# Selective scan: softplus passes on ScalarE by blocks of 512 columns instead of once over 1024

## The reference

```
xi, z = split(x @ inW.T);  u = silu(conv(xi) + convB)
dt, Bm, Cm = split(u @ xpW.T)
delta = softplus(dt @ dtW.T + dtB)            # 256 channels x 128 steps, 32 batches
A = -exp(Alog)                                # 256 channels x 16 states
h[t] = h[t-1] * exp(delta[t] * A) + delta[t] * u[t] * Bm[t]
y[t] = sum over the 16 states of h[t] * Cm[t]
out  = (y + u * Dp) * silu(z) @ outW.T
```

## Time and profile before

| | us |
|---|---|
| median of 3 runs | 3032.21 (3030.99 to 3034.59) |
| profiled execution, whole | 3035.91 |
| its span | 3033.8 |
| busy PE / DVE / ACT / POOL | 2180.6 / 2012.0 / 1294.2 / 1329.9 |

### The profile page before, as it was taken

How to read it: one execution, slowest core, us unless ns; L and a number is a source line. 1 busy time by engine, 2 the same in 40 slices (tenths; PEclk the granted TensorE clock), 3 DMA queues, 4 the chain that set the end, 5 groups by cost and what they waited for, 6 DMA issues and landing times. The chain is left out here.

```text
span 3033.8 us, 48820 instructions
## 1 busy us (share of the span) xinstructions
PE 2180.6 (72%) x19339; PEld 1337.4 (44%) x19339; DVE 2012.0 (66%) x3246; ACT 1294.2 (43%) x1935; POOL 1329.9 (44%) x1015
## 2 busy tenths in 40 slices
PE   3788766775266668998959999999999975552703
PEld 1354444554144545555525545545545543331303
DVE  3554455887444435555528888788888885888598
ACT  1344325554244422222237666666666642221460
POOL 2332243555323000000008899898898892332001
PEclk8899887887577879999979999999999997765856
DMA  3343000000343210000022222222222221000001
GB/s 90 72 77 62 10 17 31 17 17 3 73 82 75 38 47 1 1 1 1 1 62 74 71 81 80 73 75 81 78 74 73 77 63 32 21 8 8 0 0 28
DMA packets 136673, 134.58 MB, mean 44 GB/s; under 512 B 23664, under 2 KB 129920, under 8 KB 133248
## 3 DMA queue, kind: packets, MB, share of 16 engines
q1 hardware_dynamic: 136448, 131.47, 16.6%
HBM read 109.14 MB, written 15.99 MB: 41 GB/s over the span
## 5 line engine op out<-in xcount | busy, mean ns | idle before, releaser
L2154 POOL TENSOR_TENSOR mam_h<-mam_h,mam_c_all 128x1024 f32<-128x1024 f32 x256 | 658.7, 2590 | 87.9 <-DVE mam_h L2226 87.9
L2226 DVE TENSOR_TENSOR_SCAN mam_h<-mam_decay,mam_ps_b 128x1024 f32<-128x1024 f32 x256 | 574.4, 2274 | 97.2 <-PE mam_ps_b L1857 95.1
L1857 PEld LDWEIGHTS mam_ps_b<-mam_diag,mam_duT 64*128 64x128 f32 x4096 | 251.9, 190 | 219.8 <-DVE mam_h L2226 129.6
L2048 ACT ACTIVATE mam_decay<-mam_delta,mam_a_neg 128x508 f32<-128x508 f32 x512 | 331.3, 710 | 31.2 <-DVE mam_h L2226 26.9
L1857 PE MATMUL mam_ps_b<-mam_diag,mam_duT 64*128 64x128 f32 x4096 | 297.9, 287 | 55.2 <-DVE mam_h L2226 43.3
L737 DVE TENSOR_REDUCE at_top<-at_ps_s 128x8 f32<-128x1024 f32 x128 | 156.7, 1224 | 239.9 <-PE at_ps_s L483 239.7
L1876 PE MATMUL mam_ps_y<-mam_h,all_ident 64*64 64x512 f32 x2048 | 255.3, 614 | 11.9 <-POOL mam_h L2154 11.9
L620 ACT ACTIVATE at_e<-at_ps_e 128x1024 f32<-128x1024 f32 x128 | 131.2, 1025 | 194.3 <-PE at_ps_e L483 194.2
L1449 ACT ACTIVATE moe_silu<-moe_ps_g 128x512 f32<-128x512 f32 x144 | 86.0, 597 | 288.6 <-PE moe_ps_g L1396 262.2
L1399 PE MATMUL moe_ps_u<-moe_ynT,moe_w_up 128*128 128x512 f32 x288 | 158.6, 634 | 35.2 <-DVE moe_hidden L1532 35.2
L1532 DVE TENSOR_TENSOR moe_hidden<-moe_silu,moe_ps_u 128x512 f32<-128x512 f32 x144 | 96.9, 686 | 97.7 <-PE moe_ps_u L1399 94.0
(11 more groups left out here) (349 smaller groups left out, 4537.8 us busy)
## 6 DMA issues: line engine op xcount, KB each, us to landing
mam_c_all<-mam_c_rows SPq DMA_DIRECT2D x256, 256.0 KB, 3.4
at_rows<-at_split SPq DMA_DIRECT2D x64, 192.0 KB, 3.1
at_k<-at_rows SPq DMA_DIRECT2D x192, 64.0 KB
at_q<-at_rows SPq DMA_DIRECT2D x32, 192.0 KB
at_q<-at_rows SPq DMA_DIRECT2D x32, 128.0 KB
all_x_all<-in_x SPq DMA_DIRECT2D x8, 256.0 KB, 4.8
at_q<-at_rows SPq DMA_DIRECT2D x32, 64.0 KB
at_q<-at_tops SPq DMA_DIRECT2D x128, 6.0 KB
```

The costliest lines, as they stand in the source:

```text
L1857: last = nc.tensor.matmul(ps_b[:, slot, odd, :, at // 2, x:x + HT], duT[r, d, s % DT, at, :], diag[r, chunk % SLOTS, at, :, :], start=True ...
L2048: last = nc.scalar.activation(decay[:, s % SLOTS, :, n, :, 1:T], src, ACT.Exp, scale=a_neg[:, d, s % DT, st:st + 1])
L2154: nc.gpsimd.tensor_tensor(flat(h[:, slot, :, :, :, :]), flat(h[:, slot, :, :, :, :]), flat(c_all[:, chunk, :, :, :, :]), ALU.mult).then_in ...
L2226: nc.vector.tensor_tensor_scan(row(h[:, s % H_SLOTS, :, :, :, :]), row(decay[:, s % SLOTS, :, :, :, :]), row(ps_b[:, s % 2, :, :, :, :]), ...
```

## The change

For each channel block, as soon as its product is copied to `pre`, ScalarE makes Abs, Exp, the four squares and the positive part of that block (128 x 512); before, all this came once for both blocks behind the second copy. The positive part stands between the third and the fourth square instead of ahead of the first. The wait ahead of Abs for the copy is now there for each block. The exp is waited for directly ahead of the first square. ScalarE's step counter has 4 x DT counts a group instead of 4. Poly k still works on both blocks, and waits for square k of block 1.

```diff
@@ def softplus(f, steps, d, t, n)
-                if t == DT - 1:
-                    act.wait_ge(taken, f.base + f.n + ALL_TAKEN)
-                    steps.then(nc.scalar.activation(soft[:], pre[:], ACT.Abs))
-                    steps.settle()
-                    steps.then(nc.scalar.activation(soft[:], soft[:], ACT.Exp, scale=-1.0))
-                    nc.scalar.activation(pre[:], pre[:], ACT.Relu)
-                    steps.settle()
-                    for k in range(len(LOG1P_PAIRS)):
-                        nc.scalar.activation(square[:, k, :, :], soft[:], ACT.Square, bias=centre[:, k:k + 1]).then_inc(square_ready, 1)
+                act.wait_ge(taken, f.base + f.n + ALL_TAKEN)
+                steps.then(nc.scalar.activation(soft[:, t, :], pre[:, t, :], ACT.Abs))
+                steps.settle()
+                steps.then(nc.scalar.activation(soft[:, t, :], soft[:, t, :], ACT.Exp, scale=-1.0))
+                steps.settle()
+                for k in range(len(LOG1P_PAIRS)):
+                    if k == len(LOG1P_PAIRS) - 1:
+                        nc.scalar.activation(pre[:, t, :], pre[:, t, :], ACT.Relu)
+                    nc.scalar.activation(square[:, k, t, :], soft[:, t, :], ACT.Square, bias=centre[:, k:k + 1]).then_inc(square_ready, 1)
@@ def group(i, more, first=False)
-                steps = Steps(act, act_steps, i * 4 + 2, 4)
+                steps = Steps(act, act_steps, i * 4 * DT + 2 * DT, 4 * DT)
@@ def log1p(steps, n, part)
-                    dve.wait_ge(square_ready, n * len(LOG1P_PAIRS) + k + 1)
+                    dve.wait_ge(square_ready, (n * DT + DT - 1) * len(LOG1P_PAIRS) + k + 1)
```

## The result

The changed kernel is **slower by 0.64%**: ratio 1.0064, 95% interval 1.0050 to 1.0078, which is 15 to 24 us of 3033.4 (medians 3033.4 before and 3051.7 after, six runs each). The profiled execution took 3051.37 us, span 3049.2, against 3035.91 and 3033.8.

The account below looks back on a forecast made before the run. GpSimd was taken as the bound outside the softplus steps, with the chain to the first square setting when both engines go on; 2.0 + 5.5 + 4.8 + 2.0 = 14.3 us on 3032.21 gave 3046.5 us, range 3033 to 3065.

Parts of the forecast that it names:

- The chain: ScalarE's passes from copy 0 to the first square of block 1: 9.0 us against 6.97, so 2.04 us later.
- What gets through: Part of the 2.04 us shift that delays scan 9, the rest being hidden behind GpSimd's product of step 8.
- Second direction's halves: Six half groups of the pipelined loop preparing the second direction: scan 9 later by 0.34 us each, 2.0 together.
- Halves with the 4.9 us add: Five first direction's halves with the layer norm of the group before: scan 9 later by 1.1 us each, 5.5 together.
- First half: Half of the loop with poly 0 at 1622.27, taking 1.23 us, nothing hidden: +2.04 us.
- the odd halves: Four halves priced singly by poly 0's length: +2.04, +1.57, +1.2 and 0.0 us, together 4.8.
- The sum: All terms of the Mamba stage, loop halves and prologue, added: 14.3 us slower.
- The prologue: Before the loop, VectorE's wait for the first square: same longer chain, no GpSimd product to hide in, +2.0 us.
- Swallowed: Rival: VectorE's and GpSimd's collisions fall out otherwise, the time stays within 6 us, about 3035 us; chance 0.18.
- The whole shift gets through: Rival: nothing is hidden, 16 x 2.04 = 32.6 us slower, 3064.8 us; chance 0.15.
- Faster: Rival: the add ahead of the norm runs at once everywhere, shortening five halves, 3022 to 3030 us; chance 0.09.

Follow-up runs that it names:

- r3: Kernel before with one more positive part of 1024 columns ahead of the squares, not needed for the result; 1.0035 to the kernel before.
- r4: Changed kernel with two more positive parts of 512 columns in block 0, not needed for the result; 1.0107 to the kernel before.
- r8: The changed kernel itself, run again beside other kernels on the same chip; 1.0052 to the kernel before.
- r1: Kernel before with only the positive part moved behind the third square, passes whole; 1.0018 to the kernel before.
- r6: Changed kernel with the four polys a step later, behind scans 9 to 12 instead of 8 to 11; 1.0092 to the kernel before.
- r9: Changed kernel with VectorE's polys by blocks too, eight of 512 columns behind scans 8 to 11; 1.0244 to the kernel before.
- r5: Kernel before with the four polys a step later, behind scans 9 to 12 instead of 8 to 11; 1.0048 to the kernel before.
- r7: Changed kernel with each block's positive part back between Exp and the squares, so the split alone; 1.0065 to the kernel before.
- r2: Kernel before with only Abs and Exp made by blocks, squares whole, positive part whole behind the third square; 1.0017 to the kernel before.
- r10: As r9, with block 1 made and copied at step 8 instead of 7; 1.0251 to the kernel before.

## Why the prediction was right

**The chain, the term that carries all.** Forecast 9.0 us against 6.97, measured 9.02 to 9.03 in all 15 halves; passes of 512 columns took 0.61 to 0.71 us. The price from the slope of two lengths was right. The 0.3 us a pass of the Trainium skill (ScalarE: Activation LUTs, Rules for kernel authors) fits how long one such pass lasts (0.711 less 512 x 0.83 ns = 0.29); passes that follow without a wait add only 0.19 of fixed part, as the squares show (three take 1.95 us, the last of them 0.711, so each adds 0.62). For the chain the row was right, 2.05 and not 2.65 us.

**What gets through.** Second direction's halves: forecast +0.34, measured +0.35. Halves with the 4.9 us add: +1.1 and +1.09. First half: +2.04 and +2.07. Those are shown, by their rows and by r3 and r4, which moved the chain by known amounts. Of the odd halves, the one with poly 0 at 1907.05 before became an ordinary one (+1.6, forecast +1.57), the one at 1965.80 went from 10.22 to 11.43 (+1.21, forecast +1.2), and the one at 1849.35, forecast to stay, took the other variant of the add (11.41 to 13.15). That the sum held in spite of it is in part luck: two halves with a 4.9 us add before had a shorter one after.

**The sum.** Forecast for the loop 12.3 us, measured 13.8 (and 17.7 with r8's execution). The prologue: forecast 2.0, measured 3.7, from copy 0 to the first scan, 19.68 us before and 23.41 after. The chain there is 2.07; the other 1.66 us are TensorE's (below), a term I didn't have. The stages around the Mamba loop were 2.1 us shorter in this execution. 13.8 + 3.7 - 2.1 = 15.4 = 3049.2 - 3033.8. The timed runs say 15 to 24 us; my 14.3 lies just below that, and the median of 3051.7 us is 5.2 above the forecast 3046.5, so the size came out too small. 1.66 us of that were TensorE's. What the rest of a middle value of 19 is made of isn't settled: which variant a half takes differs from execution to execution, as r8's loop shows, and timed runs leave no rows. GpSimd's waits for the scan rose by 17.4 us (21.1 in r8), where I had forecast 12.

**What was wrong in the reading.** I wrote that the chain to the first square sets when both engines go on. For the second direction's halves of the kernel before this isn't so: there the product of step 8 ended 1.85 us after the first square, and the 3.6 us of VectorE's wait were not on the path. Had it been on the path, those halves of r1 would have gained by the square; they followed the product. The sum was right because the hidden part was taken off half by half; the sentence invites the wrong conclusion that a shorter chain pays. For the same reason "Swallowed" was nearer than it looks: up to about 1.7 us of delay costs nothing in six of 15 halves.

**The rivals.** "The whole shift gets through" (3064.8) fell: the two kinds of half moved by 0.35 and 1.1, not 2.04. "Faster" fell because its variant stayed rare. One half of the changed kernel (copy 0 at 2084.10) has it, an add of 1.55 us, scan 9 earlier by 1.7 us and a length of 56.4 us instead of 58.2; the kernel before has one half with such an add too. In the two with an add of 1.0 us the half before it was longer by 1.6 us (60.3 against 58.7), which eats up the 1.7 us. No scan waited for an exponential in the changed kernel, as forecast: the ones of step 10 ended 1.16 us ahead of scan 10 in the half shown (1802.66 and 1803.82). r6 shows what happens once a scan needs them earlier.

## What to carry to other kernels

If the consumer of a split pass waits for the last block, all of the first is put ahead of it, and each more pass adds its fixed part (0.1 to 0.2 us here). Splitting the consumer too takes that wait away, but need not pay: in r9 it cost far more than it gave. Before costing a wait, look at the instruction behind it: a pass of 2.9 us that takes 1.2 alone is waiting inside, for another engine, and that hidden wait is the slack that a later input may use and an earlier one can't win. Where a consumer's passes and a busy neighbour's exclude each other, cutting the consumer into dependent halves lets the neighbour in between.

## What the runs showed of the hardware

- **VectorE's polys, adds and normalizing passes and GpSimd's instructions hold each other up, and GpSimd, running back to back, mostly keeps its turn.** Poly 1.2 us alone, 2.9 behind one product, 5.08 behind a product, another and a diag (r5); GpSimd's root 1.99 instead of 1.01 behind a poly (r1). A blocked poly ended 1.08 us behind the product. Who goes next isn't fixed: the same add of 128 x 512 took 4.9 us behind a product, a diag and another product, 1.6 us where it got in ahead of the diag, and 1.0 us in other halves of one execution. The scan (one operand in SBUF, one in PSUM) ran beside products unhindered, 2.27 us on the average and at most 2.29 in both kernels. The Trainium skill (SBUF — State Buffer, SBUF: two separate sides) states such an exclusive lock, held for the whole instruction. The trace agrees as to the lock; that a waiting poly can lose the next turn too is what r5 shows. That a dependent pair of VectorE passes lets GpSimd in between (0.67 and 2.74 us, 45 times of 45 behind scans 9 to 11) is what r9 adds.
- **TensorE's clock in the prologue.** After the longer wait TensorE had been idle 3.80 us (before: 3.04), and its 32 matmuls took 3.63 us instead of 1.97. First the kernel before, then the changed one:

```profile
1590.70 1.97 PE L1840 MATMUL mam_ps_t<-all_ident,mam_du 128*64 128x128 f32 x32 [3.04 <-POOL mam_du L2135]
```

```profile
1591.03 3.63 PE L1840 MATMUL mam_ps_t<-all_ident,mam_du 128*64 128x128 f32 x32 [3.80 <-POOL mam_du L2135]
```

The mean granted clock over these 32 matmuls was 1.00 of full speed before and 0.53 after (1591.0 to 1594.66 us), so nearly all of them ran at the lower level of 1.2 GHz. The same matmuls took 3.49 to 3.68 us in r4, r6, r7, r8 and this one, after 3.8 to 4.3 us of idle time, and 1.97 in r1, r2, r5, r9 and r10, after 1.9 to 3.0. In r3 they took 2.57, at 0.74, after the same 3.04 us of idle time as before, so the length of this one wait doesn't tell it all. It happens once an execution, and put 1.66 us on top of a delay of 2.07.
